# Reusing transposed one-hots: stored by layer 0 of a two-layer graph network, loaded by layer 1, instead of computed twice

## What is computed

```python
edge_index = jnp.stack([src, dst])
h = jnp.maximum(_layernorm(x, axis=-1), 0.0)
x = x + _L0_gnn_ref(edge_index, h, Wq, Wk, Wv, gamma, beta, 8)
h = jnp.maximum(_layernorm(x, axis=-1), 0.0)
x = x + _L1_gnn_ref(h, beta1, edge_index)

# layer 0: 8 heads of 16; q from rows[e], k and v from cols[e]
att = jnp.clip(jnp.einsum('ehd,ehd->eh', qE, kE), -10.0, 10.0)
attNorm = jax.ops.segment_sum(jnp.exp(att), rows)[rows]
res = jax.ops.segment_sum((jnp.exp(att) / (attNorm + 1e-08))[..., None] * vE, rows)
# layer 1: cosine similarity, softmax with a maximum per node
alpha = jnp.sum(x[row] * x[col], axis=1) / (norm[row] * norm[col]) * beta[0]
alpha = jnp.exp(alpha - segment_max(alpha, row)[row])
out = segment_sum((alpha / segment_sum(alpha, row)[row])[:, None] * x[col], row)
```

## Time and profile before

| | |
|---|---|
| median of 3 runs | 5369.36 us (5354.42 to 5392.84) |
| the profiled execution | 5351.34 us, span of its trace 5349.6 us |
| busy in the span | TensorE 79%, its weight loads 66%, VectorE 81%, ScalarE 38%, GpSimd 64% |
| mean granted clock of TensorE | 0.767 |
| traffic | 357.55 MB, 67 GB/s on average |
| stages | sorting to 690 us, layer 0 to 2870, between the layers to 2987, layer 1 to 5326, last output to 5349 |

### The profile page before, as it was taken

How to read it: one execution, slowest core, us unless ns; L and a number is a source line. 1 busy time by engine, 2 the same in 40 slices (tenths; PEclk the granted TensorE clock), 3 DMA queues, 4 the chain that set the end, 5 groups by cost and what they waited for, 6 DMA issues and landing times. The chain is left out here.

```text
span 5349.6 us, 103650 instructions
## 1 busy us (share of the span) xinstructions
PE 4241.9 (79%) x23362; PEld 3510.8 (66%) x23363; DVE 4343.4 (81%) x12591; ACT 2006.9 (38%) x7682; POOL 3437.8 (64%) x3467
## 2 busy tenths in 40 slices
PE   5999957878787888777783588888888888888886
PEld 2788845656565666555562477777777777777776
DVE  7999968888888888888887677777877887778786
ACT  3999900000000000000004455555555555555554
POOL 0333367777777777777772576666766776666673
PEclk7999977676767666767765687887887887778786
DMA  1000033333333333333331322222222222222221
GB/s 46 17 25 22 16 90 101 101 101 102 102 101 101 101 101 102 101 101 102 101 101 38 60 52 48 50 49 47 50 50 48 50 51 48 48 47 50 47 52 49
DMA packets 172949, 357.55 MB, mean 67 GB/s; under 512 B 61770, under 2 KB 90830, under 8 KB 172690
## 3 DMA queue, kind: packets, MB, share of 16 engines
q0 software_dynamic: 136896, 330.76, 23.2%
q1 hardware_dynamic: 33958, 20.39, 1.4%
q10 hardware_dynamic: 1836, 4.03, 0.3%
HBM read 336.61 MB, written 15.12 MB: 66 GB/s over the span
## 5 line engine op out<-in xcount | busy, mean ns | idle before, releaser
L870 POOL DMA_INDIRECT h_rows<-h_table,idx_ring x1668 | 1589.5, 953 | 833.3 <-issue 479.0
L870 POOL DMA_INDIRECT kv_rows<-kv_table,idx_ring x1668 | 1652.6, 991 | 514.8 <-issue 507.7
L1047 PE MATMUL psum<-vx,hot 128*128 128x136 f32 x3336 | 865.4, 402 | 394.4 <-DVE acc L1078 375.6
L1047 PEld LDWEIGHTS psum<-vx,hot 128*128 128x128 f32 x3336 | 655.6, 270 | 589.8 <-DVE acc L1078 563.1
L1503 DVE SCALAR_TENSOR_TENSOR h_sb<-h_sb,corr,psum 128x129 f32 x1668 | 580.7, 348 | 441.5 <-PE psum L1460 169.0
L1003 ACT ACTIVATE vx<-clip 128x32 f32<-128x32 f32 x417 | 95.6, 229 | 2026.5 <-DVE clip L1118 2026.5
L1036 PE MATMUL psum<-q_sb,hotT 128*128 x3336 | 716.5, 382 | 50.1 <-DVE prod L1091 34.9
L1036 PEld LDWEIGHTS psum<-q_sb,hotT 128*128 128x128 f32 x3336 | 610.7, 274 | 193.9 <-issue 193.9
L1441 PE MATMUL psum<-q_sb,acc 128*128 x3336 | 572.7, 324 | 86.9 <-issue 86.9
L1441 PEld LDWEIGHTS psum<-q_sb,acc 128*128 128x128 f32 x3336 | 482.4, 223 | 202.1 <-issue 202.1
L1078 DVE TENSOR_TENSOR acc<-acc,psum 128x136 f32 x1668 | 485.2, 291 | 158.3 <-issue 33.4
(11 more groups left out here) (220 smaller groups left out, 5923.8 us busy)
## 6 DMA issues: line engine op xcount, KB each, us to landing
kv_rows<-kv_table,idx_ring POOLq DMA_INDIRECT x1668
h_rows<-h_table,idx_ring POOLq DMA_INDIRECT x1668
kv_table<-kv SPq DMA_DIRECT2D x21, 256.0 KB, 2.2
rows<-loc_rows SPq DMA_DIRECT2D x208, 4.0 KB
out<-q_sb SPq DMA_DIRECT2D x2, 1536.0 KB
h_sb<-h_now SPq DMA_DIRECT2D x21, 128.0 KB, 2.0
h_table<-acc SPq DMA_DIRECT2D x1, 1820.0 KB, 12.1
sorted_edges<-stage,addr POOLq DMA_INDIRECT x108, 2.9
```

Of the source, the lines that this page charges most:

```text
L870: pool.indirect_dma_start(out=G[:, u, j, :], out_offset=None, in_=table, in_offset=bass.IndirectOffsetOnAxis(ap=idx[:, u, j:j + 1], axis=0 ...
L1047: last = nc.tensor.matmul(S_ps[j // HALF][:, j % HALF, :], hot[:, k, j * P:(j + 1) * P], vx[:, k, j, :], start=True, stop=True)
```

## The change

Layer 0 stores the `hotT` of each group to a new tensor `own` in DRAM (417 x 256 KB), from SyncE, as soon as its compare is done; each of the four slots has a semaphore `s_kept` that the next compare of that slot waits for. SyncE's loads of `loc` rows are now in the same step function, behind the stores. Layer 1 has no row loads, spreads and compares any more. SyncE loads four groups of `hotT` in one transfer (1 MB) into the same ring of twelve, when L1468 of group i-9 is done, the last one that read these four slots (`s_E` has reached i - 8), and TensorE waits for the load's semaphore `s_own` where it waited for `s_hotT`. The walks of TensorE and VectorE in layer 1 begin at -1 and 0 in place of -4 and -3. The line numbers of unchanged instructions move by a few.

```diff
-def rows_of_groups(sp, ring, rows, s_spread, s_row, dram):
...
+def own_rows_of(dram, g):
+
+    return dram["own"][ds(g, 1), :, :].rearrange("o p e -> p (o e)")
@@ layer 0, SyncE
-            rows_of_groups(sp, RING0, rows, s_spread, s_row, dram)
+
+            def load_rows(first, h, n):
+                sp.dma_start(rows[0:n, h, :], dram["loc_rows"][ds(first, n), :]).then_inc(s_row[h], 16)
+
+            def step(i, u, t):
+                if inside(i):
+                    sp.wait_ge(s_hotT, i + 1)
+                    sp.sem_inc(s_go, 1)
+                    sp.dma_start(own_rows_of(dram, i), hotT[:, u % NEAR, :]).then_inc(s_kept[u % NEAR], 16)
+                    if u % FOUR == FOUR - 1:
+                        h = u // FOUR
+                        first = RING0 * t + RING0 + FOUR * h
+                        n = min(FOUR, GROUPS - first) if isinstance(t, int) else FOUR
+                        if n > 0:
+                            sp.wait_ge(s_spread, i + 1)
+                            load_rows(first, h, n)
+
+            for h in range(RING0 // FOUR):
+                load_rows(FOUR * h, h, FOUR)
+            walk(sp, step, RING0, first=0, drain=0)
+            for k in range(NEAR):
+                sp.wait_ge(s_kept[k], 16 * len(range(k, GROUPS, NEAR)))
@@ layer 0, VectorE, ahead of the compare
                     need(dve, s_q, i + 5 - NEAR)
+                    if inside(i):
+                        dve.wait_ge(s_kept[k], 16 * (RING0 // NEAR * t + u // NEAR + 1))
@@ layer 1, SyncE
-            rows_of_groups(sp, RING1, rows, s_spread, s_row, dram)
+            def step(i, u, t):
+                if u % FOUR == 0 and inside(i):
+                    n = min(FOUR, GROUPS - i) if isinstance(i, int) else FOUR
+                    need(sp, s_E, i + n - RING1)
+                    sp.sem_inc(s_go, 1)
+                    sp.dma_start(hotT[:, u:u + n, :], dram["own"][ds(i, n), :, :].rearrange("g p e -> p g e")
+                                 ).then_inc(s_own[u // FOUR], 16)
+            sp.wait_ge(s_units, 1)
+            walk(sp, step, RING1, first=0, drain=0)
@@ layer 1, TensorE
-                if inside(i + 4):
-                    need(pe, s_hotT, i + 3)
-                    spread_row(pe, nc, RING1, (u + 4) % RING1, t + (u + 4) // RING1, B_ps[u % 2],
-                               pick_row, rows, s_row, s_spread)
...
-                    pe.wait_ge(s_hotT, i + 2)
+                    pe.wait_ge(s_own[(u + 1) % RING1 // FOUR], 16 * (t + (u + 1) // RING1 + 1))
...
-            walk(pe, step, RING1, first=-4, drain=8)
+            walk(pe, step, RING1, first=-1, drain=8)
@@ layer 1, VectorE
-                if inside(i + 3):
-                    dve.wait_ge(s_spread, i + 4)
-                    need(dve, s_E, i + 4 - RING1)
-                    nc.vector.tensor_scalar(hotT[:, (u + 3) % RING1, :], B_ps[(u + 3) % 2], part_no[:, 0:1], None,
-                                            ALU.is_equal).then_inc(s_hotT, 1)
-            walk(dve, step, RING1, first=-3, drain=9)
+            walk(dve, step, RING1, first=0, drain=9)
```

More of the change, by code:

```diff
@@ L873, in gather_groups @@
     walk(pool, step, ring, first=0, drain=0)
-def rows_of_groups(sp, ring, rows, s_spread, s_row, dram):
-    parts = ring // FOUR
-    def load(t, h, n=FOUR):
-        sp.dma_start(rows[0:n, h, :], dram["loc_rows"][ds(ring * t + FOUR * h, n), :]).then_inc(s_row[h], 16)
-    for h in range(parts):
-        load(0, h)
-    with sp.Fori(1, GROUPS // ring) as t:
-        for h in range(parts):
-            sp.wait_ge(s_spread, ring * (t - 1) + FOUR * (h + 1))
-            load(t, h)
-    t = GROUPS // ring
-    for h in range(parts):
-        n = min(FOUR, GROUPS - ring * t - FOUR * h)
-        if n > 0:
-            sp.wait_ge(s_spread, ring * (t - 1) + FOUR * (h + 1))
-            load(t, h, n)
+def own_rows_of(dram, g):
+    return dram["own"][ds(g, 1), :, :].rearrange("o p e -> p (o e)")
 def spread_row(pe, nc, ring, g_u, g_t, out, pick_row, rows, s_row, s_spread):
@@ L940, in layer0_edges @@
         s_decoded = sem("s_decoded")
-        s_zero = sem("s_zero0")
         s_idx = sem("s_idx0")
@@ L953, in layer0_edges @@
         s_hotT = sem("s_hotT0")
+        s_kept = [sem(f"s_kept_{k}") for k in range(NEAR)]
         s_q = sem("s_q0")
@@ L1064, in _ @@
                                         ALU.logical_shift_right).then_inc(s_decoded, 1)
-            nc.vector.memset(acc[:, :], 0.0).then_inc(s_zero, 1)
-            dve.wait_ge(s_zero, 1)
+            link(nc.vector.memset(acc[:, :], 0.0))
             dve.wait_ge(s_part, 1)
@@ L1295, in layer1_edges @@
         slots, loc_f, blkid, cb = mem["slots"], mem["loc"], mem["blkid"], mem["cb"]
-        part_no = mem["part_no"]
         acc = mem["h"]
@@ L1303, in layer1_edges @@
         iota_j = sb("iota_j", [P, P, GT], bf16)
-        rows = sb("rows1", [FOUR, RING1 // FOUR, GE], bf16)
-        pick_row = mem["pick_row"]
         hot = sb("hot1", [P, RING1, P, GT], bf16)
@@ L1324, in layer1_edges @@
         Q_ps = [PS[:, 512 * k:512 * k + GE] for k in (0, 1)]
-        B_ps = [PS[:, 512 * k:512 * k + GE] for k in (2, 3)]
         L_ps = [PS[:, 512 * k:512 * k + GE] for k in (4, 5)]
@@ L1335, in layer1_edges @@
         s_go = sem("s_go1")
-        s_row = [sem(f"s_row1_{k}") for k in range(RING1 // FOUR)]
-        s_spread = sem("s_spread1")
+        s_own = [sem(f"s_own_{k}") for k in range(RING1 // FOUR)]
         s_locb = sem("s_locb")
@@ L1340, in layer1_edges @@
         s_hot = sem("s_hot1")
-        s_hotT = sem("s_hotT1")
         s_q = sem("s_q1")
@@ L1607, in program @@
         "loc_rows": nc.dram_tensor("loc_rows", (GROUPS, GE), bf16).ap(),
+        "own": nc.dram_tensor("own_rows", (GROUPS, P, GE), f32).ap(),
         "kv": nc.dram_tensor("kv_table", (NPAD, 2 * D), f32).ap(),
```

## The result

The changed kernel takes 5173.48 us (median of 4 runs, 5151.78 to 5175.71), against 5370.15 us for the kernel before, timed beside it (4 runs, 5354.42 to 5392.84). The ratio is 0.9622, with a 95% interval of 0.9578 to 0.9665: faster by 197 us. The forecast was 5222 in a range of 5135 to 5345. The profiled execution of the changed kernel took 5174.98 us, so profile against profile the gain is 5351.34 - 5174.98 = 176 us. The experiments were timed in several sets, each with runs of the kernel before beside them, whose median was 5357 to 5370 us but for one set; ratios are to that median, and kernels of different sets are best compared by their ratios.

The account below looks back on a forecast made before the run. Layer 0 was taken as bound by GpSimd's gather issuing, layer 1 by VectorE at full clock and TensorE at half clock. From 5351 us, minus 155 in layer 1, plus 8 for traffic: 5204, plus 18 to the median: 5222, range 5135 to 5345.

Parts of the forecast that it names:

- the low-clock step: Layer 1 at half clock, TensorE the chain: removing the spread takes 0.54 us, 6.62 to 6.08 us a group.
- the fast part: Layer 1's time outside the low clock, including 0.38 us beyond the plain step: 5.01 falls to 4.57 us a group.
- the clock's share: Share f of layer 1's time at the low clock: 0.38 before, taken as 0.45, giving 5.15 us a group.
- The plain step: Layer 1 at full clock, VectorE the chain: removing the compare takes 0.44 us, 4.63 to 4.19 us a group.
- the 0.38 on top: Layer 1: 0.38 us a group beyond the plain full-clock step, mostly the loop's stall, assumed to stay.
- The stall: VectorE at layer 1's loop branch, once per twelve groups, nothing awaited: 3.67 us (0.31 a group), forecast to stay.
- the price of the traffic: Whole kernel: 8 us added for what the extra stores and loads cost somewhere.
- the distance of the profiled execution from the median: The three timed runs' median lay 18 us above the profiled execution, so 5204 became 5222.
- the warning further down: Layer 0: if VectorE shifts against GpSimd, its collision with gathers changes: -75 us if gone, up to +139.
- rising f: Rival in layer 1: clock as in layer 0, f = 0.62, 5319 us (chance 0.14); lower still, 5484 (0.06).
- the full win of 223.6: Rival: stall gone or hidden, layer 1 at GpSimd's 4.96 us a group, -223 us, 5146; more won, chance 0.10.
- the late load: Rival in layer 1: the 1 MB load lands at 13.1 us, 5.85 a group, +137 us, 5506; chance 0.05.

Follow-up runs that it names:

- e3_stores: Kernel before with the changed layer 0, storing every group's transposed one-hots; layer 1 keeps its old code: 5403.63 us, ratio 1.0082.
- e11_before_swap: Kernel before with VectorE's sum over heads moved ahead of the product `vx` in layer 0: 5313.11 us, ratio 0.9892.
- e10_shift: Kernel before with two tiny memsets on VectorE ahead of layer 1's loop, an edit that means nothing: 5330.16 us, ratio 0.9928.
- e4_both: Changed kernel with spread and compare (to a spare tile) and the waits between them put back in layer 1; stores and loads stay: 5382.28 us, ratio 1.0055.
- e2_compare: Changed kernel with only the compare put back on VectorE in layer 1, into a spare tile: 5264.75 us, ratio 0.9826.
- e1_spread: Changed kernel with only the spread matmul put back on TensorE in layer 1, read by nobody: 5224.6 us, ratio 0.9754.
- e5_after_body24: Changed kernel with VectorE's layer-1 loop unrolled over 24 groups instead of 12, also loading block numbers in every step: 5201.56 us, ratio 0.9701.
- e8_swap: Changed kernel with VectorE's sum over heads moved ahead of the product `vx` in layer 0: 5120.28 us, ratio 0.9549.
- e12_after_shift: Changed kernel with two tiny memsets on VectorE ahead of layer 1's loop: 5159.46 us, ratio 0.9623.

## Why the prediction was right, and where it was not

**The period of layer 1 as a formula.** The prediction's groups per us, f over the low-clock step plus 1 - f over the fast part, can be held against every kernel with the clock that its window shows (f = twice what the clock lacks to 1):

| kernel | f | low, fast part | formula | measured |
|---|---|---|---|---|
| e3_stores (old code) | 0.50 | 6.62, 5.01 | 5.70 | 5.66 |
| e11_before_swap (old code) | 0.48 | 6.62, 5.01 | 5.67 | 5.67 |
| e10_shift (old code) | 0.44 | 6.62, 5.01 | 5.61 | 5.60 |
| e4_both | 0.42 | 6.62, 5.01 | 5.58 | 5.60 |
| e2_compare | 0.34 | 6.08, 5.01 | 5.33 | 5.33 |
| e1_spread | 0.34 | 6.62, 4.57 | 5.11 | 5.24 |
| after | 0.30 | 6.08, 4.57 | 4.94 | 5.10 |

The low-clock step is right (6.08 for a measured 6.07 to 6.13), and so is the fast part of the old code: 5.01 was fitted to the profile of before, and the three others with the old code, and e4_both, come out within 0.04 us. With the compare gone the fast part is 4.57 by the prediction; after gives (1 - 0.30)/(1/5.10 - 0.30/6.08) = 4.77, e1_spread 4.73 in the same way.

**The forecast held, but one step of it failed: the clock's share.** I took f = 0.45, because TensorE has less to do and the emptier layer 0 has the lower clock. It was 0.30. In the four profiled kernels whose loop has neither spread nor compare the clock is 0.85, 0.86, 0.86 and 0.85 (after, e5_after_body24, e8_swap, e12_after_shift), with one of them 0.83 and 0.83, with both 0.75 to 0.81 in six kernels: less work, higher clock. TensorE's busy share of layer 1 fell from 83% to 1585/2050 = 77% meanwhile. It is no chance of one profile: the mean clock of the whole execution was 0.752 to 0.767 in 28 timed runs of the kernel before and 0.781 to 0.790 in the four of the changed one. I had also named a clock of 0.75 to 0.80 in layer 1 as a sign of being right; 0.85 lies outside it. That the emptier layer 0 has a lower clock was a true row, but no guide to what this loop does when work is taken out. By the formula this error alone is worth (5.15 - 4.94) x 417 = 88 us.

**The fast part was mis-sized the other way,** 4.77 for 4.57, worth (5.10 - 4.94) x 417 = 67 us. The plain step is right (4.24 for 4.19); what I carried over unchanged, the 0.38 on top, grew to 4.77 - 4.24 = 0.53, by 0.15. The stall gives 3.7/12 = 0.31 of it in both kernels. Another part is the steps of 4.9 to 5.0: in the changed kernel two of them stand in nearly every loop pass, four steps apart. In the instruction order the loads of block numbers into registers come once in four groups, one of the three of a pass beside the branch, which fits these places and e5_after_body24's longer step; before, these two took 5.00 and 4.91 beside neighbours of 4.62, now they take 4.99 and 4.91 beside 4.24, so there the missing compare won nothing. Twice 0.38 in twelve steps is 0.06 of the 0.15; the rest is not settled. GpSimd's lead is not it: VectorE waited for its gathers 16 us in all.

**The sum.** 5222 - 5173.5 = 48.5 us. Of it 0.05 x 417 = 21 are the two errors above, 88 and 67 us, of opposite sign. That they nearly cancel is luck: with the clock's share right and the rest as I had it, the sum would have been 5222 - 88 = 5134, just under the range. Of the rest, 8 are the price of the traffic, which the profile comparison does not show (176 us gained, 175 of them in the period); the rest is that I added 18 us as the distance of the profiled execution from the median. That distance is the old layer 1's scatter, and the changed kernel does not have it: its profiled execution is 1.5 us over its median.

**Traffic.** e4_both costs 25 us against before, but at f = 0.42; at that f the formula, which knows of no traffic, is 0.02 us a group short, 8 us. This is what the prediction put in, but the formula misses kernels without this traffic by up to 0.04, so the price is not measured. The load was in time: one wait, 6.1 us.

**Layer 0.** Unchanged, as forecast: 991 ns a gather and 2159 us. e3_stores shows it for the stores by themselves. The compare's new wait for its store never decided: 2.3 us against four periods. The sentence that nothing done on VectorE there is worth anything was wrong, since the order of two of its instructions was worth 62 us; the warning further down, that the collision depends on how VectorE stands against GpSimd, was sound; e8_swap and e11_before_swap show its size, -62 us without the stores where I had worked out -75 as the most.

**The stall.** It stayed, 3.70 us for 3.67, and its total is 122.2 us. The Trainium skill (Runtime: NRT & Kernel Launch, Instruction fetch mechanics) has instructions fetched in blocks of 256, and a taken branch stall when its target is in neither of the two blocks that are held. The prediction took "over a block" for enough; bodies of 324 and 309 are over one block and under two, so the page alone does not decide. The trace has the stall with both, and 0.3 us with the 167 of layer 0; that fetching is its cause was not tested.

**The rivals.** The clock did not fall: rising f was a rival and half my own forecast, and both are refuted. The Trainium skill (TensorE: Matmul & The Clock Gate, What's actually happening) has activity release the full clock; TensorE got less work here and the clock went from 0.81 to 0.85, so the direction that I had drawn from it does not hold in this loop. The loads were not late. GpSimd was not reached: its wait is 57.2 us, so the full win of 223.6 was missed by about that. The times that the prediction gives for its rivals of the clock, the late load and the full win leave out the 8 us of traffic that its own sum has, which changes no conclusion.

**Why the two parts, each taken alone, add up to more than both together.** At a fixed f the spread is worth 0.54 at the low clock and the compare 0.44 at the full clock, and each removal also lowers f (0.42 to 0.34, to 0.30). The second removal finds fewer low-clock steps and, in the fast part, the steps of 4.9 to 5.0. That is what the steps and the formula show; why f falls with work on either engine was not tried.

## What to carry to other kernels

Price a removed instruction at each clock level in the chain that binds there: TensorE's matmul counted only at the low clock and VectorE's compare only at the full one, and both prices came out within 0.06 us in the plain steps. Don't carry the clock's share over from another stage; give it both signs, and measure first how far the kernel moves by an edit that means nothing, since a profiled execution is one draw from that scatter. And look at the order of instructions before judging an unrolling: here a register load that a helper repeated in each step seems to have cost more than the branch it saved.

## What the runs showed that I had not expected

- The old layer 1 has no fixed time: five executions of e10_shift lie between 5313.25 and 5370.98 us, and the same loop code shows clocks of 0.75 to 0.81 in four profiles. The changed one stays at 0.85, and its medians with and without the meaningless edit are 5159.46 and 5173.48. In one-microsecond windows the old one, in the profiled execution of before, has 101 separate low-clock stretches between 3050 and 5280 us, 14 of them longer than 16 us; the changed one has 69 up to 5105 us, about two a loop pass, none longer than 16 us.
- A VectorE product with both inputs in SBUF over the start of a gather costs layer 0 up to 62 of 2159 us, though the profile has GpSimd wait only 0.3 us for that product in all: the time of the gather tells (a mean of 991 against 954 ns, 1134 against 948 for those that meet it).
- Where four groups' block numbers are loaded into VectorE's registers, its step at the full clock is 0.39 us longer, and this shows as idle time, mostly with nothing awaited.
